# A graph network of four layers: in the last layer, one pair of edge groups in twelve is summed through a matrix built on TensorE instead of fetched rows

## What is computed

```
def _rgcn_conv(x, src, dst, edge_type, edge_weight, W, root, bias):
    xj = x[src]
    m = 0
    for r in range(4):
        m = m + (edge_type == r)[:, None] * (xj @ W[r])
    out = segment_sum(m * edge_weight[:, None], dst, num_segments=6250)
    return out + x @ root + bias

ew = (edge_weight - min) / (max - min + 1e-8)
h  = relu(_rgcn_conv(x, src, dst, type, ew, W1, root1, b1))     # pass 3
h  =      _rgcn_conv(h, src, dst, type, ew, W2, root2, b2)      # pass 4
```

## Time and the profile before

| | |
|---|---|
| median of 3 runs (range) | 4286.54 us (4285.13 to 4289.97) |
| the profiled execution: its time / its span | 4286.95 us / 4285.0 us |
| TensorE busy, mean granted clock | 2873.1 us (67%), 0.745 |
| ScalarE busy | 1801.4 us (42%) |
| VectorE busy | 1494.3 us (35%) |
| GpSimd busy | 3011.0 us (70%) |
| pass 3, first fetch to last | 2176.8 to 3215.2 us |
| pass 4, first fetch to last | 3231.9 to 4271.4 us |

### The profile page before, as it was taken

One profiled execution on the slowest core, in us unless ns is written; L12 is line 12 of the kernel. 1 busy time (PEld: TensorE's weight loads), 2 busy tenths in 40 slices (PEclk: granted clock), 3 DMA queues, 4 the chain that ended last, 5 costly groups with the idle time before them and its releaser, 6 DMA issues.

```text
span 4285.0 us, 57007 instructions
## 1 busy us (share of the span) xinstructions
PE 2873.1 (67%) x18556; PEld 2379.5 (56%) x18556; DVE 1494.3 (35%) x5844; ACT 1801.4 (42%) x4884; POOL 3011.0 (70%) x3155
## 2 busy tenths in 40 slices
PE   6999999999889997999944444444443333333333
PEld 5888888888767775666624343434343333333333
DVE  6888888888762225433310000000000000000000
ACT  1444454444341113211155555555545454444543
POOL 4777777777437773777657777777776777777776
PEclk8999999999999997999955555555555555555555
DMA  6776676766647774777622222222221222222222
GB/s 205 212 213 209 212 216 212 213 211 212 192 125 203 202 202 121 218 224 220 173 60 63 68 68 63 62 68 68 63 68 50 55 57 57 55 55 56 57 55 52
DMA packets 413114, 556.61 MB, mean 130 GB/s; under 512 B 67041, under 2 KB 287969, under 8 KB 412545
## 3 DMA queue, kind: packets, MB, share of 16 engines
q0 software_dynamic: 114112, 262.48, 22.6%
q1 hardware_dynamic: 277184, 264.23, 20.5%
q10 hardware_dynamic: 21506, 26.10, 1.8%
HBM read 450.01 MB, written 102.55 MB: 129 GB/s over the span
## 4 chain that ended last, share of the span: by engine, by line
POOL 26%; issue 9%; PE 9%; DMA 6%; ACT 0%; DVE 0%; POOLq 0%; ACTq 0%; DVEq 0%; SPq 0%
POOL work L528 26%; PE bank L1123 8%; DMA work<-table_rel,reli 6%; PE bank L1732 0%; DMA table_rel<-work 0%; ACT work L1744 0%; POOLq L595 0%; ACT work L1804 0%; PE bank L1781 0%; DVE X L1865 0%; POOLq L95 0%; PE bank L1730 0%; ACTq L1808 0%; DVE work L1155 0%; PE bank L2001 0%
## 5 line engine op out<-in xcount | busy, mean ns | idle before, releaser
L528 POOL DMA_INDIRECT work<-table_rel,reli x1664 | 1570.0, 944 | 571.5 <-issue 479.7
L1123 PE MATMUL bank<-work 128*128 128x72 f32 x3328 | 752.7, 419 | 1217.9 <-DMA work<-table_rel,reli 1217.9
L1123 PEld LDWEIGHTS bank<-work 128*128 128x128 f32 x3328 | 710.8, 324 | 1281.1 <-DMA work<-table_rel,reli 1281.1
L528 POOL DMA_INDIRECT work<-table_pre,srci x832 | 807.2, 970 | 270.9 <-issue 268.1
L1108 DVE TENSOR_TENSOR acc<-acc,bank 128x72 f32 x208 | 47.8, 230 | 1982.9 <-PE bank L1123 1982.9
L1910 ACT ACTIVATE work<-iota,local 128x72 f32<-128x72 f32 x1664 | 429.1, 341 | 402.3 <-PE bank L1123 402.3
L1915 ACT ACTIVATE work<-work,ew,src_lo 128x72 f32<-128x72 f32 x1664 | 584.8, 433 | 7.0
L1062 PE MATMUL bank<-work,acc 128*128 128x360 f16 x2574 | 437.8, 316 | 30.3 <-DVE acc L1193 18.0
L764 PE MATMUL bank<-w1a,work 128*128 128x256 f32 x1664 | 442.8, 392 | 19.9 <-DVE work L729 11.1
L528 POOL DMA_INDIRECT work<-table_mean,srci x312 | 303.7, 973 | 168.7 <-issue 88.4
L863 ACT ACTIVATE work<-work 128x512 f32<-128x512 f32 x416 | 252.0, 629 | 361.3 <-DVE work L729 359.6
(11 more groups left out here) (264 smaller groups left out, 3063.5 us busy)
## 6 DMA issues: line engine op xcount, KB each, us to landing
work<-adj SPq DMA_DIRECT2D x104, 720.0 KB
adj<-X SPq DMA_DIRECT2D x130, 450.0 KB
work<-ea_cols SPq DMA_DIRECT2D x208, 256.0 KB
work<-adj SPq DMA_DIRECT2D x52, 810.0 KB
work<-table_rel,reli POOLq DMA_INDIRECT x1664, 2.5
work<-table_pre,srci POOLq DMA_INDIRECT x832
table_rel<-work ACTq DMA_DIRECT2D x25, 512.0 KB
table_rel<-work SPq DMA_DIRECT2D x25, 512.0 KB, 2.9
```

Source lines behind the costliest of these rows:

```text
L528: pool.indirect_dma_start(into[:, u, :], None, tables[p], bass.IndirectOffsetOnAxis(ap=idx_of(p)[:, t:t + 1].bitcast(U32), axis=0)).then_i ...
L1123: mm = pe.matmul(bank[4 + n % LATE_BANKS][:, 0:PAIR_WIN], late_gat[n % LATE][:, u, :], late_hot[:, n % LATE_HOTS, u * PAIR_WIN:(u + 1) * P ...
```

## The change

In passes 3 and 4, the pairs 12, 24, ..., 96 (`D_PAIRS`, 8 of 104) are no longer fetched. Their sum over sources is formed from the node features themselves, which lie in SBUF (`X` in pass 3, the ReLU's result `h1` in pass 4). The work is cut into 80 units a pass (`D_UNITS`: 8 pairs, 2 groups each, 5 ranges of 1280 source nodes). `UNIT_AT` puts one unit at each of the places 0 to 4 and 6 to 10 of every twelve pairs (up to pair 94). For a unit:

- VectorE compares 4 code columns with a range of 480 (`unit_codes`), and for each group also makes 12 weighted one-hots of the source's low bits (three bf16 pieces of the weight).
- TensorE fills four times a PSUM bank with 3 bf16 matmuls of 480 columns (`unit_fill`), with two banks in turn.
- ScalarE copies each bank to SBUF (`unit_take`, "take" below). It does this after building the one-hots of the pair three ahead.
- TensorE multiplies node rows with it in 10 fp32 matmuls of 192 columns (`unit_use`). After 5 units ScalarE copies the group's sum out, and at the dense pair 8 fp32 matmuls of 48 columns with `W[r]` give what the fetched pair gave.

In TensorE's order a place is: fills of the unit, matmuls of the pair, block work, use of the unit. Besides: the fetch ring has 4 buffers in place of 6, the pairs' PSUM banks are 2 in place of 3, block work is spread over more places (`NODE_LAG` 5), the second relation product of a block goes through the same bank as the first, and the blocks of `h1` are transposed and copied before the block counts as done. The vote has six more small instructions and one more load.

```diff
-LATE, LATE_HOTS, LATE_BANKS, LATE_LAG, NODE_LAG = 6, 4, 3, 2, 3
+LATE, LATE_HOTS, LATE_BANKS, LATE_LAG, NODE_LAG = 4, 4, 2, 2, 5
+PERIOD = 12
+D_PAIRS = range(PERIOD, PAIRS, PERIOD)
+G_PAIRS = [h for h in range(PAIRS) if h not in D_PAIRS]
+TW = 12
+D_COLS = len(D_PAIRS) * PU
+RANGES = 5
+RHI = NT // RANGES
+CW = RELS * TW
+PIECES = 3
+D_UNITS = len(D_PAIRS) * 2 * RANGES
...
+UNIT_AT = {PERIOD * (k // (2 * RANGES)) + (0, 1, 2, 3, 4, 6, 7, 8, 9, 10)[k % (2 * RANGES)]: k for k in range(D_UNITS + 1)}
...
         def late_pool(pool, p, before):
-            for h in range(PAIRS):
-                n = (p - 3) * PAIRS + h
+            for i, h in enumerate(G_PAIRS):
+                n = (p - 3) * len(G_PAIRS) + i
                 if n >= LATE:
-                    pool.wait_ge(late_seg, n - LATE + 1)
+                    pool.wait_ge(late_seg, seg_of(n - LATE))
...
+        def unit_codes(dve, p, k):
...
+            if hr == 0:
+                for u in range(U):
+                    for i in range(PIECES):
+                        dve.tensor_scalar(late_lo[:, n // RANGES % 2, u * PIECES + i, :], iota_b[:, :],
+                                          d_lo[:, first + u:first + u + 1], d_w[i][:, first + u:first + u + 1],
+                                          ALU.is_equal, ALU.mult)
+            for u in range(U):
+                ins = dve.tensor_scalar(late_code[n % 2 * U + u], late_iota, float(hr * RHI * CW), d_code[:, first + u:first + u + 1],
+                                        ALU.add, ALU.is_equal)
+            ins.then_inc(code_ready, 1)
...
+        def unit_take(p, k, copy, eng):
+            n = (p - 3) * D_UNITS + k
+            if k and k % RANGES == 0:
+                eng.wait_ge(a_used, USES_BEFORE + n)
+                copy(d_sum[:, (k // RANGES - 1) % 2, :], bank[D_BANK][:, 0:U * CW]).then_inc(a_taken, 1)
...
+            for u in range(U):
+                eng.wait_ge(a_filled, FILLS_BEFORE + n * U + u + 1)
+                copy(late_a[n % 2][:, u, :, :].rearrange("p t c -> p (t c)"), bank[A_BANKS_AT[u % 2]][:, 0:RHI * CW]
+                     ).then_inc(a_taken, 1)
...
         def late_pe(pe, p, before, node):
             for h in range(PAIRS):
+                if unit < D_UNITS:
+                    unit_fill(pe, p, unit)
+                if h in D_PAIRS:
...
+                        for r in range(RELS):
+                            mm = pe.matmul(bank[4 + m % LATE_BANKS][:, o * U * TW:(o + 1) * U * TW].rearrange("p (u w) -> p u w", u=U),
+                                           w_rel[p - 3][:, r, :], sums[:, :, r, :], start=(r == 0), stop=(r == RELS - 1))
+                else:
...
                 mm.then_inc(late_seg, 1)
                 node(pe, h)
+                if unit < D_UNITS:
+                    unit_use(pe, p, unit)
...
+        def unit_fill(pe, p, k):
+            pe.wait_ge(code_ready, CODES_BEFORE + n + 1)
+            for u in range(U):
+                if u >= 2:
+                    pe.wait_ge(a_taken, takes_before(p, k) + u - 1)
+                elif k:
+                    pe.wait_ge(a_taken, takes_before(p, k - 1) + u + 3)
+                for i in range(PIECES):
+                    mm = pe.matmul(bank[A_BANKS_AT[u % 2]][:, 0:RHI * CW], late_lo[:, n // RANGES % 2, u * PIECES + i, :],
+                                   late_code[n % 2 * U + u], start=(i == 0), stop=(i == PIECES - 1))
+                mm.then_inc(a_filled, 1)
+
+        def unit_use(pe, p, k):
+            pe.wait_ge(a_taken, takes_before(p, k) + U)
+            rows = X if p == 3 else h1
+            for t in range(RHI):
+                mm = pe.matmul(bank[D_BANK][:, 0:U * CW].rearrange("p (u c) -> p u c", u=U), rows[:, at, :],
+                               late_a[n % 2][:, :, t, :], start=(at == 0), stop=(at == NT - 1))
...
+        def rel2_rest(pe, k):
+            pe.wait_ge(rel_emptied, emptied(1, k) + 2)
+            pe.matmul(bank[2][:, :], b_xT[:, P:2 * P], w_rel[1].rearrange("p r f -> p (r f)"),
+                      start=True, stop=True).then_inc(rel_mm, 1)
+            for j in range(BT):
+                mm = pe.transpose(bank[0][:, j * P:(j + 1) * P], b_xT[:, j * P:(j + 1) * P], ident[:, :])
...
         def late_act(act, p, first, node):
-            for h in range(PAIRS + LATE_HOTS):
-                if h < PAIRS:
+            for h in range(PAIRS + LATE_HOTS + 2):
+                if h in G_PAIRS:
...
+                if h - LATE_HOTS + 1 in UNIT_AT:
+                    unit_take(p, UNIT_AT[h - LATE_HOTS + 1], lambda to, x: act.activation(to, x, ACT.Copy), act)
```

More of the change, by code:

```diff
@@ L1098, in late_dve @@
                 dve.sem_inc(s_marks, 1)
+            if p == 3:
+                dense_setup(dve)
+            places = {}
             for h in range(PAIRS + LATE_LAG):
@@ L1107, in late_dve @@
                         dve.wait_ge(late_added, m)
-                    dve.tensor_tensor(there, there, bank[4 + m % LATE_BANKS][:, 0:PAIR_WIN], ALU.add).then_inc(late_added, 1)
-                if h >= LATE_LAG:
+                    if h - LATE_LAG in D_PAIRS:
+                        for c in range(PU):
+                            there = acc[:, 0, bass.ds(places[h - LATE_LAG][c], TW)]
+                            ins = dve.tensor_tensor(there, there, into[:, c * TW:(c + 1) * TW], ALU.add)
+                            if c + 1 < PU:
+                                done(dve, ins)
+                        ins.then_inc(late_added, 1)
+                    else:
+                        there = acc[:, 0, bass.ds(at[h - LATE_LAG], PAIR_WIN)]
+                        dve.tensor_tensor(there, there, into[:, 0:PAIR_WIN], ALU.add).then_inc(late_added, 1)
@@ new lines, in unit_codes @@
+        def unit_codes(dve, p, k):
+            n = (p - 3) * D_UNITS + k
+            pair, part = divmod(k, 2 * RANGES)
+            o, hr = divmod(part, RANGES)
+            if n >= 2:
+                dve.wait_ge(a_filled, FILLS_BEFORE + (n - 1) * U)
+            first = pair * PU + o * U
+            if hr == 0:
[8 more added lines that the diff above has]
+            ins.then_inc(code_ready, 1)
@@ L1114, in late_pe @@
         def late_pe(pe, p, before, node):
             slow_pe(pe, p, before)
-            for h in range(PAIRS):
-                n = (p - 3) * PAIRS + h
-                pe.wait_ge(late_gathered[n % LATE], (n // LATE + 1) * 16 * PU)
-                pe.wait_ge(late_ready, n + 1)
-                if n >= LATE_BANKS:
-                    pe.wait_ge(late_added, n - LATE_BANKS + 1)
-                for u in range(PU):
-                    mm = pe.matmul(bank[4 + n % LATE_BANKS][:, 0:PAIR_WIN], late_gat[n % LATE][:, u, :],
-                                   late_hot[:, n % LATE_HOTS, u * PAIR_WIN:(u + 1) * PAIR_WIN], start=(u == 0), stop=(u == PU - 1))
+            if p == 3:
+                pe.wait_ge(n2_step, len(UNITS) * 4)
+                pe.wait_ge(rel_emptied, emptied(0, BLKS))
+            else:
+                pe.wait_ge(rel_emptied, emptied(1, BLKS))
@@ new lines, in late_pe @@
+            for h in range(PAIRS):
+                m = (p - 3) * PAIRS + h
+                unit = UNIT_AT.get(h, D_UNITS)
+                if unit < D_UNITS:
+                    unit_fill(pe, p, unit)
+                if h in D_PAIRS:
+                    pe.wait_ge(a_taken, takes_before(p, unit))
+                    pe.wait_ge(late_added, m - LATE_BANKS + 1)
+                    for o in range(2):
+                        sums = d_sum[:, o, :].rearrange("p (u r w) -> p u r w", u=U, r=RELS)
+                        for r in range(RELS):
+                            mm = pe.matmul(bank[4 + m % LATE_BANKS][:, o * U * TW:(o + 1) * U * TW].rearrange("p (u w) -> p u w", u=U),
+                                           w_rel[p - 3][:, r, :], sums[:, :, r, :], start=(r == 0), stop=(r == RELS - 1))
+                else:
+                    n = (p - 3) * len(G_PAIRS) + G_PAIRS.index(h)
+                    pe.wait_ge(late_gathered[n % LATE], (n // LATE + 1) * 16 * PU)
+                    pe.wait_ge(late_ready, n + 1)
+                    if m >= LATE_BANKS:
+                        pe.wait_ge(late_added, m - LATE_BANKS + 1)
+                    for u in range(PU):
+                        mm = pe.matmul(bank[4 + m % LATE_BANKS][:, 0:PAIR_WIN], late_gat[n % LATE][:, u, :],
+                                       late_hot[:, n % LATE_HOTS, u * PAIR_WIN:(u + 1) * PAIR_WIN], start=(u == 0), stop=(u == PU - 1))
@@ L1955, in node3_root @@
                 pe.wait_ge(n2_sum, len(UNITS) + k)
-            pe.matmul(bank[7][:, 0:BLK], w_root[0][:, :], b_v, start=True, stop=True).then_inc(n3_root, 1)
+            pe.matmul(bank[1][:, 0:BLK], w_root[0][:, :], b_v, start=True, stop=True).then_inc(n3_root, 1)
         def node3_pe_at(pe, g):
@@ L2016, in node4_act, with node @@
         def node4_act(act):
-            late_act(act, 4, lambda: None, lambda k: norm_root(act, n2_step, n2_root, len(UNITS) + k, 0, BT))
+            def node(g):
```

(3 more changed lines are left out.)

143 lines of the change are left out of this document (116 added, 27 removed).

## The result

| | before | changed |
|---|---|---|
| median (range), runs taken together | 4288.26 us (4285.13 to 4292.00, 4 runs) | 4151.35 us (4146.04 to 4153.29, 4 runs) |
| the profiled execution: time / span | 4286.95 / 4285.0 us | 4150.75 / 4148.9 us |
| TensorE, mean granted clock | 0.745 | 0.919 |

The ratio is 0.9678 (95% interval 0.9662 to 0.9695), 137 us less. The forecast was 4173 us, and its range holds the result. But pass 3 was forecast to be paced by the loop through the takes, and it was not: fetches pace both passes, which is the outcome of the first rival (4135 us). In pass 3 it is close: fetches and loop take the same time within 1%.

The account below looks back on a forecast made before the run. Fetches were taken to bound passes 3 and 4. From 4286.95 us, less 47 (pass 3) and 79.9 (pass 4), plus 4 for fetches, 2.6 between passes, 1.3 start and 5 hand-overs, it forecast 4173 us, range 4130 to 4240.

Parts of the forecast that it names:

- the first rival: Fetches pace passes 3 and 4, needing a loop below 9.15 us a place in pass 3; 4135 us, chance 0.15.
- Fetches pace both passes before: Passes 3 and 4 of the kernel before: 1.248 us a fetch, 9.99 us a pair of 8, nothing else near.
- Cost of a unit on TensorE: Fills 2.5 us, use 3.5, the pair's matmuls 1.85: 7.9 us a place at full clock, 15.6 at half.
- The clock: TensorE's clock rises in places with a unit, falls in the two without; 7 us per twelve places.
- The loop: One-hots, two takes, last fill, pair's matmuls in series: 8.8 us a place, 105 us per twelve with the clock.
- So pass 3 is paced by this loop: Pass 3: loop 105 plus block work 12.1 is 117.1 us per twelve places; gain 47 us.
- Pass 4 paced by fetches: Pass 4: fetches, 109.8 us per twelve places, still set the pace; gain 79.9 less 4 for longer fetches.
- Between the passes: Between passes 3 and 4: the second product waits for the first one's copy, transposes behind it; +2.6 us.
- The start: The vote gets six steps of about 0.2 us, +1.3; its new load hides or costs up to 3 us.
- Hand-overs: Uncounted hand-overs of 160 units, 0.05 us each in pass 3; +5 us.
- The second: Rival: the loop is 0.6 to 1 us longer a place; 4261 us, range 4215 to 4290, chance 0.17.
- the third: Rival: TensorE stays at half clock in most places and is itself the bound; 5150 us, chance 0.10.

Follow-up runs that it names:

- less_8_pairs_again: Kernel before without the fetches of the eight pairs in passes 3 and 4, their matmuls multiplying the identity; 4934.28 us, ratio 0.9657, on a chip with standstills.
- before_small_rings: Kernel before with 4 fetch buffers in place of 6 and 2 PSUM banks for pairs in place of 3; 5037.89 us, ratio 0.9964, chip with standstills.
- half_fetches: Changed kernel fetching only 4 of the 8 tiles of each fetched pair in passes 3 and 4; 4422.20 us on a chip with standstills.
- changed_again: The changed kernel as it is, timed again as a reference on the undisturbed chip; 4151.82 us, ratio 0.9683.
- no_compares: Changed kernel with nearly all VectorE compares for codes and small one-hots left out in passes 3 and 4; 5162.88 us, ratio 1.022, chip with standstills.
- one_pass_compares: Changed kernel with code and small one-hot compares made by scalar_tensor_tensor, code column broadcast as second input; 5309.09 us, ratio 1.0413, chip with standstills.
- period_10_one_pass: Changed kernel with one dense pair in ten, a unit at every place, and scalar_tensor_tensor compares; ratio 1.050, on a chip with standstills.

## Why the prediction was right, and where it was not

- **Fetches pace both passes before**: right; less_8_pairs_again keeps the step of 1.248 us.
- **Cost of a unit on TensorE**: right. Use matmuls 0.34 us (0.35 taken), fills 0.23 (1.38 us for six rows of fills; 0.21 taken), the pair's 1.90 (1.85).
- **The clock**: right in kind. It rises in the filled places and falls in the free ones. Over passes 3 and 4 it is 0.91 and 0.85 (0.8 to 0.9 forecast). The price of one fall was right where it could be read place by place (3.0 + 0.6 us), but per twelve places the two falls cost 4.6 to 5.4 us and not 7.
- **The loop**: its chain is right, its length too high: 8.6 us for 8.8, 5.1 for 5.5 in a free place, 7.8 for 8.0 in the place that builds no one-hots, and there are two places of that length in twelve (9 and 10), not one. Twelve places are 99.1 for 105. Of these 5.9 us the clock and the ordinary places are some 2 each.
- **"So pass 3 is paced by this loop", at 117.1**: this step failed, by the size of the loop's terms. Measured are 112.0, of which the block work (12.9 for 12.1) is not the error; it is the 5.9 us of the bare loop. Since the fetches have become longer, their own pace is 111.0, and the ring's lead takes the rest. The prediction's sum had no term for that lead in pass 3. It was to gain 47 us and gained 68.9.
- **Pass 4 paced by fetches**: right, 79.9 less 4 forecast, 70.0 measured. The lengthening of a fetch was sized at 5 ns, by the load of VectorE in pass 0, and is 14: the term of 4 us should have been 11, in both passes. The rule named in that step, from the Trainium skill (SBUF — State Buffer, Who interferes with whom), agrees with the traces in its direction. The scaling by busy time failed: a few fetches that catch a run of compares lose 0.6 us each, and nearly all others lose nothing.
- **Between the passes** +4.7 for +2.6: the root product behind the last pair was missed. **The start** +1.4 for +1.3; the new load landed in time. **Hand-overs** +5: none where fetches set the pace.
- **Sum**: 4173, less 22 in pass 3, plus 6 in pass 4, plus 2 between, less 5, less 3 of passes 0 to 2, is 4151. The errors were of both signs, and the largest is the failed step. That 4173 is only 22 us off is in part luck, for the longer fetches took back some of what the shorter loop gave.

Of the rivals, the first gives what happened, but not by its own conditions: it needs a clock that doesn't fall or a loop less chained, below 9.15 us a place in pass 3. The clock fell, the chain is as drawn, and the loop alone takes 9.33 us a place. Its outcome came by smaller terms, longer fetches and the ring's lead. Its sum is 4135, 16 us below the result, and 13 of these are fetches (21 us of lengthening, where it had counted 8). The second (longer takes or use) and the third (half clock) didn't come.

## What to carry to other kernels

Where two loops are within a few per cent of each other, the one that paces can't be named from a sum of terms read to 0.1 us; say what each gives, and remember that a ring's lead hides an excess of some us over a whole pass. Before moving work onto VectorE beside GpSimd's indirect DMAs, ask how many of these will meet a run of its instructions without gaps, and look at the longest fetches in the trace, not at VectorE's share of busy time or the mean fetch. A budget found this way (8.6 us of work in a place of 10) can be spent: one pair in ten gave 20 us more.

## What was not expected of the hardware

On two of three chips the kernel before takes 5056.19 us (13 runs) and 5108.96 us (7 runs) in place of 4285.82. Timeline of before_small_rings, pass 3 ("remote" is what the trace can't name):

```profile
2984.44 2.81 ACT L1915 ACTIVATE work<-work,ew,src_lo 128x72 f32<-128x72 f32 x8
...
2988.89 0.60 ACT L1910 ACTIVATE work<-iota,local 128x72 f32<-128x72 f32 x2 [0.17 <-issue]
...
2995.92 2.81 ACT L1915 ACTIVATE work<-work,ew,src_lo 128x72 f32<-128x72 f32 x8 [6.43 <-remote]
...
2999.39 0.51 ACT L1936 ACTIVATE work<-work,bias 128x256 f32<-128x256 f32 x1 [0.66 <-issue]
...
3007.23 1.19 PE L1730 MATMUL bank<-work,w_all 128*128 128x256 f32 x2 [22.97 <-remote]
3007.28 0.23 DVE L1108 TENSOR_TENSOR acc<-acc,bank 128x72 f32 x1 [22.79 <-remote]
3007.93 0.94 POOL L528 DMA_INDIRECT work<-table_rel,reli  x1 [4.94 <-remote]
```

TensorE shows 23 us without work. It is not alone. Its next product (L1730) needs ScalarE's ReLU (L1936), which ends at 2999.90, and starts 7.3 us after that; and ScalarE had itself stood still for 6.43 us between two of its own instructions (L1910 and L1915), of which the second waits for nothing but the first. On the undisturbed chip this gap is 0.03 us in all 207 pairs of the kernel before; in before_small_rings it is over 0.5 us in 47 of 207, up to 9.5. So a part of what looks like TensorE's standstill is ScalarE's. GpSimd then waits 4.94 us for a buffer; 38 such gaps of about 4 us fall in this pass. In passes 3 and 4 of this run TensorE has 51 gaps of over 15 us, in the kernel before on the other chip one, between the passes. In passes 0 to 2 it is many pieces of a few us.

In half_fetches no gap of over 15 us is left within passes 3 and 4, with the same matmuls in them as in the changed kernel, so the standstills don't simply come with instructions, as changed_again had supposed. With the full fetches the kernels with more TensorE work fared worse: no_compares, which gains 3.6% undisturbed, loses 2.2% there, and one_pass_compares and period_10_one_pass lose 4.1% and 5.0%, in part by their longer fetches. Whoever carries this change over should time it on more than one chip. What stops the engines stays open; single fetches and matmuls are as long as on the undisturbed chip (0.944 to 0.947 us for a fetch that meets nothing).
